# Routing ranks ahead of the first feed-forward part, attention steps ahead of its last outputs, and an earlier normalisation inside attention

## What is computed

```python
x = x + 0.5 * ffn(layernorm(x))      # FFN 1
x = x + attention(layernorm(x))      # 16 heads of 8, softmax, projection
x = x + 0.5 * ffn(layernorm(x))      # FFN 2, the same weights
```

```python
gate_v, gate_o = sel_gate(x, sel_v_w), sel_gate(x, sel_o_w)   # sigmoid, top 2 of 8 per head, weights normalised
v   = einsum('bshep,bshe->bhsp', einsum('bsd,hedp->bshep', x, v_w), gate_v)
att = softmax(q @ k.T / sqrt(128))
ctx = att @ v
out = einsum('bshep,hepd->bsd', ctx * gate_o, o_w)            # 8 experts per head
```

## Time and profile before

| | us |
|---|---|
| median of 3 runs | 1533.58 (1531.26 to 1534.4) |
| the profiled execution | 1530.61 |
| its span, first to last instruction | 1528.8 |
| TensorE busy | 1469.9 (96%) |
| VectorE busy | 1277.4 (84%) |
| ScalarE busy | 1206.7 (79%) |
| GpSimd busy | 988.5 (65%) |
| granted TensorE clock, mean | 0.99 of 2.4 GHz |

### The profile page before, as it was taken

How to read it: one execution, slowest core, us unless ns; L and a number is a source line. 1 busy time by engine, 2 the same in 40 slices (tenths; PEclk the granted TensorE clock), 3 DMA queues, 4 the chain that set the end, 5 groups by cost and what they waited for, 6 DMA issues and landing times.

```text
span 1528.8 us, 25886 instructions
## 1 busy us (share of the span) xinstructions
PE 1469.9 (96%) x7263; PEld 1104.6 (72%) x7263; DVE 1277.4 (84%) x3381; ACT 1206.7 (79%) x3603; POOL 988.5 (65%) x1752
## 2 busy tenths in 40 slices
PE   7899999999999999979989999999999999999997
PEld 5677888888888788743333358887888788888885
DVE  6999889988988877788878848988898889888875
ACT  4788888888888888738887888888888788888885
POOL 4588877777777677652351236777677767776665
PEclk9999999999999999999999999999999999999999
DMA  6234533322243225302211013333233333333321
GB/s 201 85 126 149 193 138 111 111 110 104 105 141 108 102 105 207 116 23 71 93 59 56 15 69 125 111 111 110 96 109 109 110 116 111 111 111 117 111 83 35
DMA packets 50837, 163.48 MB, mean 107 GB/s; under 512 B 3460, under 2 KB 26630, under 8 KB 34310
## 3 DMA queue, kind: packets, MB, share of 16 engines
q1 hardware_dynamic: 50694, 161.82, 30.2%
HBM read 136.64 MB, written 25.17 MB: 106 GB/s over the span
## 4 chain that ended last, share of the span: by engine, by line
PE 47%; DVE 6%; ACT 2%; issue 1%; POOL 1%; POOLq 0%; ACTq 0%; DVEq 0%
PE bank L535 10%; PE bank L536 10%; PE bank L537 10%; PE bank L702 3%; PE bank L850 3%; DVE mmax L1489 3%; PE bank L815 3%; PE bank L717 2%; PE bank L715 2%; PE bank L716 2%; DVE ot L1379 1%; PE bank L835 1%; ACT ot L1058 0%; PE bank L860 0%; PE bank L824 0%
## 5 line engine op out<-in xcount | busy, mean ns | idle before, releaser
L1019 ACT ACTIVATE vt<-bank,gate 128x128 f32<-128x128 f32 x1024 | 293.1, 374 | 104.0 <-PE bank L537 89.9
L1379 DVE SCALAR_TENSOR_TENSOR ot<-bank,gn,ot 128x128 f32<-128x128 f32 x1024 | 287.8, 343 | 70.8 <-ACT ot L1058 52.6
L1644 POOL TENSOR_TENSOR vt<-vt 128x256 f32<-128x256 f32 x256 | 197.2, 770 | 220.1 <-DVE vt L1365 219.1
L1058 ACT ACTIVATE ot<-bank,gn 128x128 f32<-128x128 f32 x1024 | 291.9, 372 | 24.7 <-PE bank L537 17.3
L1365 DVE SCALAR_TENSOR_TENSOR vt<-bank,gate,vt 128x128 f32<-128x128 f32 x1024 | 285.8, 341 | 11.6 <-ACT vt L1019 9.4
L1670 POOL TENSOR_TENSOR ot<-ot 128x256 f32<-128x256 f32 x252 | 194.7, 773 | 88.0 <-DVE ot L1379 84.2
L1392 DVE TENSOR_TENSOR pt<-bank,pt 128x512 fp32r<-128x512 f32 x256 | 175.5, 685 | 69.7 <-ACT pt L1046 69.3
L535 PE MATMUL bank<-wv,xhl 128*128 128x512 f32 x512 | 224.1, 438 | 3.0 <-DVE vt L1365 2.1
L535 PE MATMUL bank<-wo,chl 128*128 128x512 f32 x512 | 206.1, 403 | 6.2 <-DVE chl L1348 4.9
L1035 ACT ACTIVATE pp<-bank,nmin 128x512 f32<-128x512 f32 x256 | 178.2, 696 | 42.5 <-DVE nmin L1355 40.6
L1355 DVE TENSOR_REDUCE nmin<-bank 128x1 f32<-128x512 f32 x256 | 173.4, 677 | 37.1 <-PE bank L537 33.7
(11 more groups left out here) (195 smaller groups left out, 2998.5 us busy)
## 6 DMA issues: line engine op xcount, KB each, us to landing
wv<-wv_split SPq DMA_DIRECT2D x56, 1024.0 KB, 4.8
wo<-wo_split SPq DMA_DIRECT2D x56, 1024.0 KB, 4.8
wv_split<-wv SPq DMA_DIRECT2D x8, 1024.0 KB, 5.1
wo_split<-wo SPq DMA_DIRECT2D x8, 1024.0 KB, 7.1
qk<-qk_rows SPq DMA_DIRECT2D x32, 256.0 KB, 2.8
qk_rows<-qs SPq DMA_DIRECT2D x24, 256.0 KB, 2.9
rawv<-in_L_ffn_v_w SPq DMA_DIRECT2D x8, 512.0 KB, 6.2
rawo<-in_L_ffn_o_w SPq DMA_DIRECT2D x8, 512.0 KB, 8.2
```

What stands on the lines that cost most here:

```text
L1019: last = activation(vt[:, u % 2, e * P:(e + 1) * P], gb[0][:, e * P:(e + 1) * P], ACT.Copy, scale=gate[:, n % 2, k, h * E + e:h * E + e + 1])
L1058: last = activation(ot[:, u % 2, e * D:(e + 1) * D], output_bank(f, i, 0)[:, e * D:(e + 1) * D], ACT.Copy, scale=gn[:, j % 2, k, e:e + 1])
L1379: last = v.scalar_tensor_tensor(o, output_bank(f, i, 1)[:, e * D:(e + 1) * D], gn[:, j % 2, k, G + e:G + e + 1], o, ALU.mult, ALU.add)
L1644: own.link(g_.tensor_tensor(a[:, 0:2 * P], a[:, 0:2 * P], a[:, 2 * P:4 * P], ALU.add))
```

## The change

Three places change. **Prologue.** GpSimd's two splits of the value weights move: the first waits until VectorE has added the 1 (`one_added`), the second until the gates are there (`gates_in`), and the rests of the attention weights `wqs` and `wks` move to slot 72. VectorE subtracts the rest of `mh` behind the gates, and the output half's reciprocal is cut into four, one in each of the slots -3 to 0. `query(0)` of FFN 1 moves from slot -3 to slot -1, and the products with no use are 22 instead of 36. Of the weights of heads 2 to 7, GpSimd subtracts the second half (slot 3 of each head) where VectorE did. **FFN 1's tail.** In slots 125 to 134 the outputs and the context products of a slot (`ending`) are issued behind the attention steps of that slot, on every engine. **Inside attention.** Statistics for FFN 2 at step 156 instead of 160 (so GpSimd's `normalise` at 162 instead of 166), the transposition at 172, logits at 178, ranking from 200.

```diff
@@ constants
-IDLE_PRODUCTS = 36
+FIRST_QUERY = (-1, -V_AHEAD)
+IDLE_PRODUCTS = 22
-AGAIN, TURN_AGAIN, LOGITS_AGAIN, RANK_AGAIN = 160, 170, 176, 198
+AGAIN, TURN_AGAIN, LOGITS_AGAIN, RANK_AGAIN = 156, 172, 178, 200
@@ schedule
         s += STEPS_BESIDE.get(at, 0)
+        if at in STEPS_BESIDE:
+            order.append((3, at))
@@ every engine's slot
-                    if t == -V_AHEAD:
+                    if t == FIRST_QUERY[f]:
                         query(0)
...
-                    if 0 <= t - O_BEHIND < TILES:
-                        outputs(t - O_BEHIND, 0)
-                        outputs(t - O_BEHIND, 1)
-                    for c in CONTEXT_BLOCKS[k] if 1 <= g <= HEADS else ():
-                        context(g - 1, c)
+                    if not (f == 0 and t in STEPS_BESIDE):
+                        ending(t)
@@ VectorE, prologue
-            own.link(v.tensor_scalar_add(pr, pr, 1.0))
+            v.tensor_scalar_add(pr, pr, 1.0).then_inc(one_added, 1)
+            dve.wait_ge(one_added, 1)
             own.link(v.reciprocal(xn[:, :, 0:HE], xn[:, :, 0:HE]))
+            for s in range(PICKS):
+                first_pick(0, s, best_masked)
+            dve.wait_ge(setup_copied, 1)
...
+            first_weights(0, best_picked, gates_in)
             for h in range(2):
                 dve.wait_ge(mh_hi, h + 1)
...
-            for s in range(PICKS):
-                first_pick(0, s, best_masked)
-            own.link(v.reciprocal(left[:, :, 0:HE], xn[:, :, HE:]))
@@ VectorE, slot
+                    if f == 0 and t <= 0:
+                        own.link(v.reciprocal(left[:, t + V_AHEAD, 0:HE], xn[:, t + V_AHEAD, HE:]))
...
-                    if f == 0 and k >= 2 and 0 <= g < H - 2:
-                        split_values(g + 2, k - 2)
+                    if f == 0 and k == 2 and 0 <= g < H - 2:
+                        split_values(g + 2, 0)
@@ GpSimd
-            split_values(0)
...
-            split_values(1)
-            pool.wait_ge(mha_hi, 1)
-            for w, whole in ((wqs, wqf), (wks, wkf)):
...
+            pool.wait_ge(one_added, 1)
+            split_values(0)
...
             pick_first(0, best_masked, best_picked)
+            pool.wait_ge(gates_in, 1)
+            split_values(1)
...
+                    if f == 0 and k == 3 and 0 <= g < H - 2:
+                        split_second(g + 2)
                     if t + V_AHEAD < TILES:
                         fold_values(t + V_AHEAD)
```

85 lines of the change are left out of this document (55 added, 30 removed).

## The result

The changed kernel takes **1516.65 us** (median of 3 runs, 1516.36 to 1516.67), the kernel before 1533.58. The ratio is 0.9897, with a 95% interval of 0.9882 to 0.9912: 16.9 us faster by the medians, where 16.6 us and 1517 us were forecast. A second comparison on another chip gave 1517.91 against 1532.75, ratio 0.9918 [0.9895, 0.994]: 14.8 us.

The account below looks back on a forecast made before the run. TensorE, busy without a break in the feed-forward parts from 130 us, was taken as the bound, with gains only where it waits: prologue -4.6, tail -6, normalisation -6, together -16.6 us from 1533.58 to 1517, range 1511 to 1527.

Parts of the forecast that it names:

- The open step: Prologue: GpSimd's first split ends at 15.5 if bias rows run earlier, otherwise 16.8, holding a pick; 0.3 us allowed.
- rival 3: Heads 2 to 7: GpSimd becomes the bound through the added splits, up to 7.8 us lost, 1525 us; chance 0.06.
- What the prologue gives back: Behind the gates: moved query 0.5 us, rest of `mh` 0.15, reciprocal quarters the remainder; together 1.2 us lost.
- The moved halves: Value-weight splits: VectorE loses 0.68 us of work each, worth 0.7 us once and 0.3 for the other five together.
- what is gained is kept as a shift: Whole kernel: TensorE is the bound behind each of the three places, so gains last to the end, -16.6 us.
- part A: Prologue: earlier gates -4.8, given back 1.2, moved halves -1.0; sum -4.6 us, between -2.5 and -6.5.
- B: Tail of FFN 1: row maxima no longer stand behind VectorE's wait for ScalarE's outputs; -6 us, between 0 and -8.
- The two new waits: Tail, TensorE: step 6 waits 1.3 us for bank 4, step 20 waits 1.25 us for a maximum.
- Rival 1: Tail no faster: TensorE's waits behind scores eat VectorE's gain, so nothing gained there; 1523 us, chance 0.14.
- Rival 4: Tail falls to the lower clock: all its upper-level work at the lower one, +16 us there, 1539 us; chance 0.03.
- C: Inside attention: earlier normalisation and later transposition remove TensorE's 3.25 us wait for x; -6 us, between -3.25 and -8.
- Rival 2: Attention: the wait turns into another on bank 5, so only -2 us gained there, 1521 us; chance 0.13.

Follow-up runs that it names:

- a_splits_early: Changed kernel with GpSimd's two prologue splits of the value weights back ahead of the picks: 1519.68 us, ratio 0.9933 to the kernel before.
- a_halves_dve: Changed kernel with the second halves of the value weights of heads 2 to 7 split on VectorE again: 1517.07 us, ratio 0.9897 to the kernel before.
- p_prologue: Kernel before with only the prologue's change, including the second halves moved to GpSimd: 1528.33 us against 1533.39, ratio 0.9966.
- p_tail: Kernel before with only the tail's change, outputs and contexts of slots 125 to 134 behind the attention steps: 1528.24 us, ratio 0.9964.
- p_tail_again: Same kernel as p_tail, the kernel before with only the tail's change, run once more for a second trace: 1530.02 us (one run).
- p_norm: Kernel before with only the attention steps moved to 156, 172, 178, 200 (statistics, transposition, logits, ranking): 1526.11 us, ratio 0.996.
- after_again: The changed kernel unaltered, run again to see its spread: six executions from 1516.6 to 1526.7 us.
- a_beside: Changed kernel with attention steps spread 2, 2, 2, 4, 3, 3, 3, 4, 4, 4 over slots 125 to 134: 1520.73 us, ratio 0.9921 to the kernel before.
- a_turn_late: Changed kernel with the statistics back at step 160, transposition still at 172: 1516.98 us, ratio 0.991 to the kernel before.
- a_norm_early: Changed kernel with statistics at 156 but transposition, logits and ranking back at 170, 176, 198: 1522.48 us, ratio 0.9938 to the kernel before.

## Why the prediction was right

The forecast, 1517 us by the median, was met to 0.4 us. That agreement is better than the working behind it, so here it is step by step.

**The gates and the first product: right.** Gates at 22.2, measured 22.32; first product at 23.45, measured 23.62, 4.67 us earlier than before instead of 4.8. The open step, whether the bias rows could run earlier, came out on the better side (12.14), and the first split (13.43 to 15.78) met the reciprocal, which took 1.75 us as before, and a reduction. So the 0.3 us set aside for it weren't needed. About as much went elsewhere: from the end of the picks to the end of the gates it takes 2.1 us instead of 1.85, because GpSimd's masking, which had run beside the output half's reciprocal, now runs beside `gsum`, and that takes 0.55 us instead of 0.18 (0.55 in `a_splits_early` too). The prediction named this meeting and gave it no price. The two slips cancel, and 22.2 is in that part luck. That GpSimd's splits were what had lengthened the add and the pick was an argument from neighbours in time; `a_splits_early` shows it, by bringing the slow add back and a slow step among the picks. The rule of the Trainium skill that was weighed in rival 3 (SBUF — State Buffer, Who interferes with whom) fits here: an instruction with both inputs in SBUF and a split of GpSimd exclude each other, and the later one, begun 0.7 us into the split, ended only 0.28 us behind the split's end. Rival 3's 0.27 us for such a meeting was misread, though: the split at 57.65 in the earlier trace rows was over before VectorE's 0.95 us began at 60.90. What stood beside that was GpSimd's `vv` (60.65 to 61.31), and the split behind it was itself held up, to 1.74 us instead of 1.30 (before, GpSimd):

```profile
61.27 1.74 POOL L1632 TENSOR_TENSOR wo<-rawo,wo 128x512 fp32r<-128x512 f32 x1
```

**What the prologue gives back: 1.2 us forecast, and slot 0 shows 4.7 - 4.1 = 0.6 us of it.** The quarters of the reciprocal take 0.54 us each, not 0.44, because a quarter of an instruction isn't a quarter of its time. Up to slot 6 the advance shrinks to 3.2 us, as far as VectorE is the bound; there the whole 1.5 us has gone.

**The moved halves: mis-sized.** They were to be worth 0.7 us in the first heads and 0.3 us behind, and to stay. `a_halves_dve` has them at 1.3 us in slot 12 and at 0.2 us in slot 124. The step that failed is "what is gained is kept as a shift": part A's 5.0 us at slot 12 are 4.3 at slot 30 and 3.5 at slot 124 (and 5.0 and 3.8 in `p_prologue`), in a stretch where TensorE is busy almost throughout, and no wait grows enough to name it. A good part of it is only the spread between executions: from slot 12 to slot 124 before took 544.5 us, the shortest of all fourteen traces, and after 545.9, the longest. The other four traces without moved halves (`p_tail`, `p_tail_again`, `p_norm`, `a_halves_dve`) took 544.7 to 545.3, the other eight with them 545.1 to 545.7. By the means that leaves about 0.6 us to the moved halves, 0.4 of it between slots 24 and 40 (78.1 to 78.2 us against 77.7 to 77.8). Why they cost that there is open. By the traces A was -3.5, against -4.6; by the medians of `p_prologue`, -5.1. Both lie within -2.5 to -6.5.

**The tail: right, and in the middle for the reason given.** B was -6, measured 9.3 - 3.5 = 5.8 us in the profiled pair (5.9 by the length of the window), 4.8 by all the traces and 5.2 by the medians of `p_tail`. About 1 us of the pair's 5.8 is thus which executions were profiled. The two new waits were put at 1.3 and 1.25 us and are 1.27 and 1.57. VectorE is busy for 91% of the window, where over nine tenths were expected: 3.5 us are idle, between the 2 us of my layout and what hand-overs would cost. Rival 1, no gain, is ruled out: up to step 8, 16.6 us in before, the new order takes 12.2 in the changed kernel and in `p_tail`, both at the full clock, and 13.2 in `after_again` with 3.4 us at the lower one, as before has. Rival 4, the clock, is a real mechanism; it shows in `p_tail`, in `p_tail_again` and in `a_beside`, but it took 4.4 and 2.9 us in the first two, not 16. It was sized as if all of the work ran at the lower level, and the most that any trace shows inside the tail is 10.2 us of it, in two stretches.

**The normalisation: right.** C was -6, measured 6.4 in the pair, 16.0 us for steps 168 to 184 as forecast, clock 1.00. The short waits in this stretch come to 1.47 us, but 0.86 were there before, so the change added 0.6 where 0.5 was put for bank 5. Rival 2 is ruled out by the 6.4 us. The gain is about half the wait (3.25 us) and, as what is left over, half the clock that had fallen behind it: 10.2 us at the lower level in before, from 798.0 on, where after has none. The margin was mis-sized: four steps earlier plus two later were counted as 4.8 us, but from 3.25 us short it went to 6.3 us to spare, some 9.5 in all. GpSimd's work starts 6.6 us earlier by the work around it, where four steps make 3.2, because it also comes out from behind `oN` and `qk`, which the prediction named and gave no time; the transposition is due some 2.9 us later, where two steps make 1.6. So either move alone all but removes the wait (`a_turn_late`, `a_norm_early`), and the two are not both needed.

**What was not foreseen:** "distances from step 184 on should be as before". They are, up to slot 128. There the clock falls behind a wait that both kernels have, and 1.5 us go. It happens in most traces with part C in them, though not in those of `a_halves_dve` and `a_norm_early`; it doesn't in before, `p_prologue` and the first trace of `p_tail`, but `p_tail_again`, without part C, has it (at 898.4). So what decides it stays open.

**Luck in the last digit.** The profiled execution came out 2.4 us above its own forecast, 1514.0: 1.1 us from part A, 0.2 from part B and 1.5 from the clock at slot 128, less 0.4 that part C gained over its estimate; smaller differences elsewhere cancel. The median nevertheless met 1517, because I counted 3 us between the profiled execution of before and its median, and after has only 0.3 us there. The second comparison, with 14.8 us between the medians, would have put it 2 us off. Twenty runs of before spread from 1530.08 to 1537.4 us; its profiled execution was one of the fastest.

## What to carry to other kernels

When an engine with two inputs from SBUF takes several times its usual time once, look what GpSimd does at that moment; moving GpSimd's work behind the critical chain is then worth about the excess. Where one engine is the bound only in a short stretch (a tail, the first slots), lay out its queue there and put the work that waits for nobody in front of the work that waits; but count the slots in which a bank is used for the fourth time: four of them instead of two (`a_beside`) made 7.5 us of waits out of 2.8. A wait of 3 us on TensorE can cost twice its length through the clock behind it, and single traces of the same kernel differ by several us for that reason, so judge a part that is worth 5 us by medians and use the trace for where, not for how much.

## What the runs showed of the hardware that I had not expected

- **The granted clock falls at other places in other executions of one kernel.** `p_tail` had it low from 660.8 for 6.8 us and from 674.5 for 3.4, `p_tail_again` from 656.1 for 3.4 and from 673.2 for 6.8, with the same waits ahead. `a_norm_early` had it low for 30.7 us without a break, with TensorE busy for 29.45 of them, and lost 10 us. The time follows the mean granted clock: in `after_again` 1516.6 us at 0.994 and 1526.7 at 0.984, in the 20 runs of before 1530.08 at 0.991 and 1537.4 at 0.986.
- **A low clock can cost less than half its length**: 3.4 us of it cost 0.2 us in the tail of `a_turn_late` and 1.1 in that of `after_again`. TensorE alone would lose half of the stretch, 1.7 us. VectorE is nearly the bound in this tail, and that is the likely reason; no run isolates it.
- **Some VectorE instructions and GpSimd's exclude each other for a whole instruction.** A tensor_tensor of 128x256 took 2.04 us instead of 0.42, beside a GpSimd subtraction of 2.46 us; a tensor_scalar of 128x512, with only one tensor as input, took 0.80 instead of 0.43. Both ended 0.28 us behind GpSimd's end. Others are free of it: in `a_splits_early` a tensor_reduce beside the same subtraction took its 0.42 us. A reciprocal of 128x256 took 1.75 us with the split beside it (after) and without (before), and the Trainium skill, same section, says as much: with one input in SBUF and outside the two-port modes there is no contention.
- **Small pieces of VectorE's reciprocal are dear**: 0.54 us for 128x64 where 128x256 takes 1.75, so four quarters cost 2.16.
- **An advance can melt where nothing waits**: 5.0 us at slot 12 were 3.5 at slot 124. The same 112 slots take 544.5 to 545.9 us from trace to trace, so more than half of this melting is spread; some 0.6 us go with the moved halves, and their cause is open.
